# Running key-value states masked inside their scan and multiplied in 32x32 tiles, in an attention block with a quantised FFN

## The reference

```
x = x + attn(layernorm(x))         # 32 sequences, 512 tokens, 256 features
x = x + ffn(layernorm(x))          # 256 -> 1024 -> 256, silu

# attn, per sequence and head (16 heads of 16 features), in chunks of 128 tokens:
q, k = elu(x Wq + bq) + 1, elu(x Wk + bk) + 1 ;  v = x Wv + bv
num = tril(q k^T) v + q S          # S: sum of k^T v over the earlier chunks
den = sum(q * (cumsum(k) + z))     # z: sum of k over the earlier chunks
out = num / den ;  S += k^T v ;  z += sum(k)
return out Wo + bo
```

## Time and profile before

| | |
|---|---|
| median of three runs | 1494.43 us (1490.52 to 1497.98) |
| the profiled execution | 1494.15 us |
| its span, from the first to the last instruction | 1492.1 us |
| PE busy | 1414.1 us (95%) |
| DVE busy | 1233.3 us (83%) |
| ACT busy | 1036.8 us (69%) |
| POOL busy | 793.0 us (53%) |
| mean granted clock of TensorE | 0.98 |

### The profile page before, as it was taken

How to read it: one execution, slowest core, us unless ns; L and a number is a source line. 1 busy time by engine, 2 the same in 40 slices (tenths; PEclk the granted TensorE clock), 3 DMA queues, 4 the chain that set the end, 5 groups by cost and what they waited for, 6 DMA issues and landing times.

```text
span 1492.1 us, 64840 instructions
## 1 busy us (share of the span) xinstructions
PE 1414.1 (95%) x27482; PEld 1231.5 (83%) x27482; DVE 1233.3 (83%) x2077; ACT 1036.8 (69%) x1789; POOL 793.0 (53%) x469
## 2 busy tenths in 40 slices
PE   7669999999999999999999999999999999999978
PEld 7558888888888888888888888888888888888857
DVE  5678888888889888888988888988888898888774
ACT  4357777766777876777776677787677778667643
POOL 2124566545566645456654556664545665455443
PEclk8779999999999999999999999999999999999989
DMA  5111011111101111101111110111110111111010
GB/s 155 38 44 57 25 38 50 56 56 56 52 16 47 54 56 56 56 28 35 50 56 56 56 50 18 47 54 56 56 56 28 35 49 56 56 56 39 11 41 29
DMA packets 83299, 72.13 MB, mean 48 GB/s; under 512 B 14912, under 2 KB 82752, under 8 KB 83264
## 3 DMA queue, kind: packets, MB, share of 16 engines
q1 hardware_dynamic: 81904, 71.62, 15.6%
q10 hardware_dynamic: 1360, 0.01, 0.1%
HBM read 38.03 MB, written 16.78 MB: 37 GB/s over the span
## 4 chain that ended last, share of the span: by engine, by line
PE 78%; DVE 11%; issue 7%; ACT 2%; POOL 1%; DMA 0%; DVEq 0%; ACTq 0%; POOLq 0%
PE sc L287 24%; PE ring L287 18%; PE num L287 6%; DVE state L644 5%; PE sc L408 5%; DVE probs L627 4%; PE sc L353 4%; PE sc L354 3%; PE num L455 2%; PE ring L353 2%; PE ring L394 2%; PE num L335 2%; PE ring L427 2%; ACT silu_f L832 2%; PE ring L354 1%
## 5 line engine op out<-in xcount | busy, mean ns | idle before, releaser
L982 POOL TENSOR_TENSOR s_lo<-silu_f,s_hi 128x512 fp32r<-128x512 f32 x256 | 416.1, 1631 | 565.4 <-ACT s_hi L847 562.2
L840 ACT ACTIVATE silu_f<-silu_f 128x512 f32<-128x512 f32 x256 | 156.4, 622 | 77.1 <-DVE silu_f L617 76.2
L627 DVE TENSOR_TENSOR probs<-sc,causal 128x1024 f32<-128x1024 f32 x128 | 150.8, 1220 | 31.3 <-PE sc L408 31.2
L888 ACT ACTIVATE hn<-x,hn_add,ln_rstd 128x256 f32<-128x256 f32 x128 | 66.5, 591 | 152.9 <-DVE hn_add L736 152.9
L832 ACT ACTIVATE silu_f<-sc,bias,scale 128x512 f32<-128x512 f32 x155 | 120.1, 776 | 63.8 <-PE sc L354 63.6
L847 ACT ACTIVATE s_hi<-silu_f 128x512 fp32r<-128x512 f32 x256 | 158.7, 621 | 1.1
L644 DVE TENSOR_TENSOR state<-kv_sums,head_ones 128x896 f32<-128x896 f32 x64 | 144.5, 2303 | 0.0
L287 PE MATMUL sc<-w_hi,s_hi 128*128 128x256 f32 x496 | 142.8, 288 | 0.0
L353 PE MATMUL sc<-gt_hi,w_q 128*128 128x512 f32 x286 | 122.8, 429 | 21.1 <-DVE probs L627 21.1
L287 PE MATMUL ring<-w_hi,s_lo 128*128 128x256 f32 x496 | 139.9, 282 | 0.0
L287 PE MATMUL ring<-w_hi,s_hi 128*128 128x256 f32 x496 | 139.9, 282 | 0.0
(11 more groups left out here) (186 smaller groups left out, 4270.0 us busy)
## 6 DMA issues: line engine op xcount, KB each, us to landing
x_in<-in_x SPq DMA_DIRECT2D x32, 512.0 KB, 4.0
rb<-den_rows SPq DMA_DIRECT2D x512, 32.0 KB, 1.9
xb<-in_x SPq DMA_DIRECT2D x32, 512.0 KB, 4.7
out<-out_t SPq DMA_DIRECT2D x64, 256.0 KB, 2.4
probs<-in_q SPq DMA_DIRECT2D x2, 512.0 KB, 8.4
silu_f<-in_q SPq DMA_DIRECT2D x2, 512.0 KB, 6.4
res<-in_sc SPq DMA_DIRECT2D x1, 512.0 KB, 6.8
out_t<-in_sc SPq DMA_DIRECT2D x1, 512.0 KB, 9.3
```

What stands on the lines that cost most here:

```text
L627: masked.done(e.tensor_tensor(probs[:, t, 2 * h:2 * h + 2, :, :, :].rearrange("p g m a q -> p (g m a) q"), sc[:, 2 * h:2 * h + 2, :].rearr ...
L840: silu.done(e.activation(slot, slot, ACT.Silu))
L982: sl.done(e.tensor_tensor(s_lo[:, j, :], silu_f[:, j % SLOTS, :], s_hi[:, j, :].bitcast(F32), ALU.subtract))
```

## The change

The scan's operands change places. It was (keep x running sum) + bank; it becomes (running sum + bank) x keep, with `keep` zero at the last of each group of eight blocks, and zero for all columns of the other head of the pair. So the running sum comes out masked, as `state` (128x512), and there are no snapshots and no second tile. `from_states` uses it in place: the stationary operand of pair g is 32 partitions by 32 columns, read from `state` with a step of eight elements (32 bytes) between columns, and the moving operand is 32 partitions of `phi_q`; both t wait for the one event `summed`, with a `hold` ahead.

The denominators become eight matmuls of 128 columns: for each chunk m a group of 32 PSUM rows, into which both t are summed with a `head_one` that has the heads of its t in its own eight columns (each twice) and zeros elsewhere. The reciprocal is over 128x128, and eight DMAs, each from eight rows that it repeats 16 times, fill `rb`.

```diff
-        head_one = sb("head_one", [P, 32])
-        scan_keep = sb("scan_keep", [P, S])
+        head_one = sb("head_one", [P, T, 2, T, HT])
+        state_keep = sb("state_keep", [P, S])
...
-        den_rows = sb("den_rows", [P, 2 * P])
+        den_rows = sb("den_rows", [P, P])
...
-        kv_sums = sb("kv_sums", [P, S])
-        state = sb("state", [P, T, STATES, P])
+        state = sb("state", [P, S])
...
-        kv_view = kv_sums[:, :].rearrange("p (t x c) -> p t c x", t=T, c=2 * C)
+        state_view = state[:, :].rearrange("p (t x c) -> p t c x", t=T, c=2 * C)
...
             def from_states(t):
-                w.need(snap, 0, t)
+
+                w.need(summed, 0)
+                w.hold()
                 for c in range(1, 2 * C):
                     m, r = divmod(c, 2)
                     for g in range(PAIRS):
-                        last = e.matmul(num[PW * g:PW * (g + 1), r, num_of(r, t, m)],
-                                        state[:, t, c - 1, PW * g:PW * (g + 1)], phi_q[:, t, chunk(r, m)],
+                        pair = slice(PW * g, PW * (g + 1))
+                        last = e.matmul(num[pair, r, num_of(r, t, m)],
+                                        state_view[pair, t, c - 1, :], phi_q[pair, t, chunk(r, m)],
                                         start=False, stop=False, skip_group_check=True)
...
                 for t in range(T):
-                    for half in range(2):
-                        g = 2 * t + half
-                        last = e.matmul(use_bank("den")[32 * g:32 * g + 32, 0:2 * P], head_one[:, :],
-                                        qk[:, t, 2 * P * half:2 * P * (half + 1)], start=True, stop=True,
+                    for m in range(C):
+                        last = e.matmul(use_bank("den")[32 * m:32 * m + 32, 0:P], head_one[:, t, :, :, :],
+                                        qk[:, t, m * P:(m + 1) * P], start=(t == 0), stop=(t == T - 1),
                                         skip_group_check=True)
...
-                kv_sb.done(e.tensor_tensor_scan(kv_sums[:, :], scan_keep[:, :], use_bank("kv"), 0.0, ALU.mult, ALU.add))
-
-            def snapshots(t):
-                if not A:
-                    return
-                w.need(kv_sb, 0)
                 w.need(num_pe, -1)
-                shape = [P, STATES, PAIRS, PW]
-                snap.done(e.tensor_tensor(
-                    state[:, t, :, :].rearrange("p n (g x) -> p n g x", x=PW),
-                    kv_view[:, t, 0:STATES, :][:, :, None, :].to_broadcast(shape),
-                    head_ones[:, :].rearrange("p (g x) -> p g x", x=PW)[:, None, :, :].to_broadcast(shape), ALU.mult))
+                summed.done(e.tensor_tensor_scan(state[:, :], use_bank("kv"), state_keep[:, :], 0.0, ALU.add, ALU.mult))
...
-                rden.done(e.reciprocal(den_rows[:, :], use_bank("den")[:, 0:2 * P]))
+                rden.done(e.reciprocal(den_rows[:, :], use_bank("den")[:, 0:P]))
...
-            snapshots(0)
-            snapshots(1)
...
                 for t in range(T):
-                    for half in range(2):
-                        g = 2 * t + half
-                        for a in range(DUP):
-                            e.dma_start(rb[a:P:DUP, t, 2 * P * half:2 * P * (half + 1)], den_rows[32 * g:32 * g + 32, :])\
-                                .then_inc(rb_in.sem, 16)
+                    for m in range(C):
+                        rows = den_rows[32 * m + t * HT:32 * m + (t + 1) * HT, :]
+                        e.dma_start(rb[:, t, m * P:(m + 1) * P], rows[:, None, :].to_broadcast([HT, HD, P]))\
+                            .then_inc(rb_in.sem, 16)
```

More of the change, by code:

```diff
@@ L75, in build @@
     SLOTS = 4
-    DUP = 32 // HT
     WARM, WARM_BETWEEN = 22, 5
@@ L216, in build @@
         half_pe, upd_pe = ev("half_pe", 1), ev("upd_pe", 1)
-        kv_sb, snap = ev("kv_sb", 1), ev("snap", T)
+        summed = ev("summed", 1)
         sc_pe, masked, av_pe = ev("sc_pe", T), ev("masked", 2 * T), ev("av_pe", T)
         num_pe = ev("num_pe", 1)
-        den_pe, rden, rb_in = ev("den_pe", 1), ev("rden", 1), ev("rb_in", 1, step=16 * 2 * T * DUP)
+        den_pe, rden, rb_in = ev("den_pe", 1), ev("rden", 1), ev("rb_in", 1, step=16 * T * C)
         attn, at_h, at_l = ev("attn", T), ev("at_h", T), ev("at_l", T)
@@ L245, in build @@
             "ht0": (ht_l, 0), "ht1": (ht_l, 1), "kt0": (kt_sb, 0), "kt1": (kt_sb, 1), "sc0": (masked, 1), "sc1": (masked, 3),
-            "xt0": (xt_l, 0), "xt1": (xt_l, 1), "kv": (kv_sb, 0), "num": (attn, 1),
+            "xt0": (xt_l, 0), "xt1": (xt_l, 1), "kv": (summed, 0), "num": (attn, 1),
             "k0": (phi, 0), "q0": (phi, 1), "k1": (phi, 2), "q1": (phi, 3), "v0": (v_sb, 0), "v1": (v_sb, 1),
@@ L1059, in build @@
         V_QK, V_W1, V_BIAS_O, V_BETA, V_W2, V_BIAS_2 = 2, 3, 4, 5, 6, 7
-        CONSTS = 17
+        CONSTS = 21
         def stage_of(n):
@@ L1111, in _ @@
             e.wait_ge(p_const, CONSTS)
-            e.wait_ge(p_par, 1)
+            e.wait_ge(p_par, 2)
             ac_iteration(e, -1, False, False, True, True)
@@ L1132, in _ @@
             count(e.memset(ones[:, :], 1.0))
-            for tile_, value in ((head_ones, 1.0), (causal, 1.0), (causal_2, 1.0), (head_one, 1.0)):
-                count(e.memset(tile_[:], value))
+            for tile_, value in ((head_ones, 1.0), (causal, 1.0), (causal_2, 1.0)):
+                count(e.memset(tile_[:, :], value))
+            count(e.memset(head_one[:, :, :, :, :], 0.0))
+            e.wait_ge(p_const, made)
+            for t in range(T):
+                count(e.memset(head_one[:, t, :, t, :], 1.0))
             count(e.memset(minus_half[:, :, :], -0.5))
@@ L1146, in _ @@
             select(blocks, ALU.is_ge, HD - 1, [[HD, HT], [0, HD]], -1, 0.0)
-            copies = head_one[:, :].rearrange("p (h x) -> p h x", x=DUP)
-            select(copies, ALU.is_ge, 0, [[-HD, HT], [0, DUP]], 1, 0.0)
-            select(copies, ALU.is_ge, HD - 1, [[HD, HT], [0, DUP]], -1, 0.0)
+            for t in range(T):
+                select(head_one[:, t, :, t, :], ALU.is_ge, 0, [[0, 2], [-HD, HT]], 1, 0.0)
+                select(head_one[:, t, :, t, :], ALU.is_ge, HD - 1, [[0, 2], [HD, HT]], -1, 0.0)
             select(causal[:, :], ALU.is_ge, 0, [[1, HALF]], -1, 0.0)
@@ L1175, in projections @@
                 e.tensor_scalar(bias_qkm[:, :, :], bias_qk[:, :, :], -1.0, None, ALU.mult).then_inc(p_v, 1)
-            e.memset(scan_keep[:, :], 1.0).then_inc(p_par, 1)
-            e.wait_ge(p_par, 1)
-            e.memset(scan_keep[:, 0:S:2 * C], 0.0)
+            e.memset(state_keep[:, :], 1.0).then_inc(p_par, 1)
             early(e, ht_l, f_b, e_out, res_m)
-            e.wait_ge(p_const, 10)
+            e.wait_ge(p_const, 12)
             e.tensor_reduce(out=parity[:, :], in_=head_ones[:, :].rearrange("p (g a x) -> p a g x", a=2, x=HD)[:, :, :, 0],
@@ L1185, in _ @@
             ve_norm_x(e, Waiter(e, -1), 1)
+            e.wait_ge(p_par, 2)
+            own = state_keep[:, :].rearrange("p (t a y) -> p t a y", t=T, a=2)
+            e.tensor_tensor(own, own, parity[:, None, :, None].to_broadcast([P, T, 2, S // (2 * T)]), ALU.mult)\
+                .then_inc(p_par, 1)
+            e.wait_ge(p_par, 3)
+            e.memset(state_keep[:, 2 * C - 1:S:2 * C], 0.0).then_inc(p_par, 1)
             def weights_1():
@@ L1201, in _ @@
             ve_iteration(e, -1, False, False, True, True, (projections, None, weights_1, None))
+            e.wait_ge(p_par, 4)
             e.wait_ge(p_pe, 1)
@@ L1227, in _ @@
         def _(e):
-            e.wait_ge(p_const, 8)
+            e.wait_ge(p_const, 10)
             early(e, ht_pe, f_pe, z_pe)
```

## The result

The changed kernel takes **1758.04 us** (1750.96 to 1764.72), the one before 1492.73 (1490.52 to 1497.98): the ratio is 1.1771, with an interval of 1.171 to 1.1831. The forecast was 1486.2, and nothing in its range comes near. The profiled execution took 1764.72 us, with a span of 1763.0.

A forecast was written before the change was run, and what follows sets the result against it. It took PE's own instructions as the bound, with DVE's snapshots adding a 0.3 us wait. Terms -9.0 + 0.6 + 0.3 + 0.2 = -7.9 us against the profiled 1494.15 gave 1486.2 us, range 1480 to 1497.

The forecast's parts named there:

- 4 matmuls of 256 columns become 8 of 128: Denominators on PE: two added steps, a couple of ns each, 0.01 us a batch, +0.3 us in all.
- The first and last batches gain nothing: Batches at both ends: PE waits there for its own instructions, up to 3.7 us at a time, not for DVE.
- if PE's from_states row is longer than before, the load is what I priced too low: Sign in the trace after: a longer row of from_states' 112 matmuls would mean strided loads cost more than 0.
- Rival 3: from_states slower: loads don't hide, 1533 us, or tiles sharing a bank take turns, 1639; 12%, 2 of them the bank.
- The snapshots' wait, -9.0: from_states: PE's wait for DVE's second snapshot, 0.3 us each, 28 times, goes away: -9.0 us.
- 32x32 tiles at 0: from_states: four 32x32 tiles with strided loads take 57 ns as before, so the change there costs 0.
- rival 1: from_states: strided loads show a little, a step of 61 to 67 ns, 3.6 to 9 us, 1490 to 1495; 14%.
- The limit of 33 ns: from_states: a load of up to 57 / 1.7 = 33 ns stays hidden at DVE's ratio for the stride.
- The hold: Ahead of from_states on PE: a handover longer by 0.02 us a batch, +0.6 us in all.
- the reciprocal: Denominators on DVE: 128 instead of 256 columns, 1.76 to about 0.9 us, worth 0 because of slack behind it.
- the transfers: DMAs filling `rb`: SP issues 8 instead of 16, about 5 us instead of 10, worth 0.
- The start: Start of the launch: added DVE and POOL instructions, mostly within existing waits, +0.2 us, between 0 and 0.8.

The follow-up runs named there:

- Run 8: Kernel before with only the denominators' part of the change, and 6 warming matmuls of 512 columns for 22 of 128 ahead of the loop: 1494.81 us.
- run 1: Changed kernel with 6 warming matmuls of 512 columns for 22 of 128 ahead of the loop, 64 fewer TensorE instructions: 1489.7 us, ratio 0.9975.
- run 9: Kernel before with only the denominators' part of the change, the 22 warming matmuls ahead of the loop left as they were: 1733.48 us.
- run 3: Kernel before with 26 warming matmuls for 22 ahead of the loop, 16 more TensorE instructions: 1799.82 us, ratio 1.2044.
- run 2: Kernel before with 6 warming matmuls of 512 columns for 22 of 128 ahead of the loop: 1841.83 us, ratio 1.2356.

## Why the prediction was wrong, step by step

**The step that failed.** "4 matmuls of 256 columns become 8 of 128 [...] 0.01 a batch, +0.3 us". That prices the added matmuls by their time on the array, and there it is right: the place is as long as before, 0.65 us for 0.64 at the same 0.71 us to the reciprocal's start:

```profile
655.33 0.65 PE L467 MATMUL sc<-qk,head_one 128*32 128x128 f32 x16
656.04 0.96 DVE L655 RECIPROCAL den_rows<-sc 128x128 f32<-128x128 f32 x1 [1.14 <-PE sc L467]
```

(Run 8, whose loop is undisturbed.) What has no term in the sum is the instructions themselves, 52 up to the loop's end, 48 of them from this step and 4 from the holds. By the count of places nine would have been free; all 52 cost 268 us. In its place: 28 passes x (53.60 - 43.90) = 272 us, the difference between the spans of after and of run 1 (272.1).

**The sentence that should have led there.** "The first and last batches gain nothing: there PE waits for its own instructions ('issue', up to 3.7 us at a time [...])". The row was read, and the next question not asked: why do those batches wait for their instructions, and the 28 between them not? The answer was in the DMA queues of the page: the packets of the instruction queue stop at 117.9 us and start again at 1367.3. The loop lived off code that stayed, and there is a limit to that.

**The sign that would have misled.** The prediction ends: "if PE's from_states row is longer than before, the load is what I priced too low". In the changed kernel it is longer: from its first matmul to its last 3.78 us, against 1.91 before (medians). The load is not what did it, since run 1 has the same loads and 1.73. What tells the two apart is in the rows: one pause of 2.11 us inside the block, and not a longer step all through it.

**The rivals.** Rival 3 named 1533 and 1639 us, for slow loads and for a shared bank. Both are measured away by run 1: 1489.7. That the slower side had 12% was no help, since none of it was this mechanism.

**The snapshots' wait, -9.0: right.** No wait of from_states for DVE is left. Before, 0.371 us lay between the starts of the last matmul of the first half and the first of the second; with packed loads it is 0.036. With them from_states is 1.552 us where it was 1.91, 0.36 a batch and 10.0 in 28. DVE's busy time fell by 158.5 us in run 1, for "some 170" forecast.

**32x32 tiles at 0: wrong in size; rival 1 is what happened.** The text put "a step of 61 to 67 ns instead of 57" at 14% and 1490 to 1495 us. The step is 62.5 ns, of which packing gives back 6.6: 0.182 us a batch, 5.1 us in 28. DVE's ratio of 1.7 for the same stride, which was on the table, was a fair warning. The limit of 33 ns that the text drew from it gave none: the recorded load grew from 105 to 141 ns, 1.34 times, and that was enough to show. The Trainium skill (SBUF — State Buffer, in "Door 1: The DMA port swizzle") asks for two hits in a line, fp32 at a step of 4 at most; the measurement sides with it against my 0.

**The hold, the reciprocal, the transfers: worth what was forecast.** The last matmul of values starts near 675.72 + 1.48 - 0.23 = 676.97 in run 1 and from_states at 677.13, a handover of 0.16 for the 0.15 to 0.17 given. The reciprocal takes 0.96 us for "about 0.9". The eight transfers take 7.27 us to issue in the changed kernel (7.39 in run 1), 0.91 each, not the 5 us of the text:

```profile
714.71 7.27 SPq L1017 DMA_DIRECT2D rb<-den_rows  x8
```

At zero worth that costs nothing, as stated. The start can't be read: in run 1 from_states of the third batch begins at 150.04 us, before at 150.52, but run 1 has other warming matmuls too, so the 0.2 us stay open.

**The sum, undisturbed.** The loop of run 1 is faster by 28 x (44.066 - 43.904) = 4.5 us for the 7.9 forecast, and the median by 3.6; the strided loads' 5.1 are the shortfall, give or take 1 or 2 us. The profiled spans differ by only 1.2 us: what lies around the 27 periods is 3.2 us longer than before. Those batches fetch their code in every version, and the borders fall elsewhere in them when code is moved; that this is the cause was not tried.

## What to carry to other kernels

Before a change to a loop of many small instructions, look at the instruction queue in the page and at when its packets come: none within the loop means that it lives on the chip, and then count its instructions on that engine, and where it starts. An edit that adds a few, in the loop or ahead of it, can cost 18%, though run 1 shows the same instructions at full pace; and an "issue" wait at the same matmul in every pass, with close to a multiple of 256 instructions between such places, is its sign. When parts of a change are tried by themselves, hold the place of the code fixed (here by fewer, wider warming matmuls), or the part that carries the loop over the border is blamed for what it doesn't do.

## What the runs showed of the hardware

- TensorE's loop ran from the chip while it and the piece fetched behind it were within 8 pieces of 256 instructions, and fetched all 9 in every pass when they were not: 27 against 280 packets of 16.4 KB, 9.7 us an iteration here (8.5 in run 9, 10.9 in run 3, 12.1 in run 2).
- The edge is a few instructions wide: 1791 of 1792 no pass lost, 1795 two passes of 28, 1799 all.
- In the pass shown, pieces of small tiles were entered 3.5 and 3.9 us apart with a pause before the next (737.27, 740.74, 744.67), and pieces of large matmuls, 12 to 14 us long, without one. The granted clock was 0.50 from 746.06 to 749.40, behind pauses of 0.86 and 2.11 us, and 0.94 over the pass, where PE's busy time grew by 4.1 us beside 5.5 us of added idling.
- In the same pass a packet of code started 3.1 us after a piece was entered where the DMA engines were busy for 0.82 with the kernel's loads, and 0.8 to 1.3 us after it in the next four pieces, where they were nearly idle.
- A 32x32 stationary tile read at every eighth fp32 loads in 141 ns, packed in 105, and four of its matmuls then take 62.5 and 55.9 ns. Packed tiles of 32 rows are as fast as tiles of 128 rows: in the kernel before, the second half of from_states took 0.770 us from its first matmul to its last, 56 ns for four.
